# Edge network kernel: z of even and odd quarters in the two row halves of the array, sums behind all of z

## The reference

```python
h = jnp.maximum(_layernorm(x), 0.0)                       # 6250 x 64
msg_in = concat([h[src], h[dst], edge_attr_32], axis=-1)  # 206250 x 160
messages = silu(msg_in @ W1 + b1) @ W2 + b2
att = softmax(silu(msg_in @ Wa1 + ba1) @ Wa2 + ba2, axis=0)   # over all edges
agg = segment_sum(messages * att, dst, 6250)
out = x + silu(concat([h, agg], -1) @ Wu1 + bu1) @ Wu2 + bu2
```

## Time and profile before

| | |
|---|---|
| median of 3 runs | 2449.22 us (2447.33 to 2454.1) |
| profiled execution: span | 2482.0 us |
| profiled execution: its own time beside the span | not on record |
| POOL busy | 1529.9 us (62%) |
| PE busy, PEld busy | 1101.1, 963.4 us |
| DVE busy | 1086.6 us |
| ACT busy | 919.5 us |
| chain that ended last | issue 48%, PE 33%, DVE 9% |

### The profile page before, as it was taken

The page is one execution under the profiler, slowest core; times in us unless marked ns, Lnnn a source line. Parts: engine busy times, 40 slices in busy tenths (PEclk is TensorE's granted clock), DMA queues, the critical chain, the costliest instruction groups (busy, mean ns, idle before and its releaser), DMA issues.

```text
span 2482.0 us, 21022 instructions
## 1 busy us (share of the span) xinstructions
PE 1101.1 (44%) x6767; PEld 963.4 (39%) x6767; DVE 1086.6 (44%) x2367; ACT 919.5 (37%) x1107; POOL 1529.9 (62%) x1628
## 2 busy tenths in 40 slices
PE   4334444444444444444444444444444444444447
PEld 3223343444333333444333334343433333444444
DVE  4344444444444444444444444444444444444445
ACT  3333333334333333334333333343433333333433
POOL 4666666666666666666666666666666666666650
PEclk8566666666666666666666666666666666666766
DMA  7433333333333333333333333333333333333321
GB/s 202 106 90 90 90 89 88 92 91 95 98 93 88 90 88 88 90 93 90 99 95 89 89 90 89 87 94 89 98 95 91 89 90 90 87 93 90 95 65 27
DMA packets 101990, 228.43 MB, mean 92 GB/s; under 512 B 45184, under 2 KB 65460, under 8 KB 91636
## 3 DMA queue, kind: packets, MB, share of 16 engines
q1 hardware_dynamic: 47588, 120.63, 18.5%
q0 software_dynamic: 51584, 105.75, 17.2%
q10 hardware_dynamic: 2704, 0.66, 0.1%
HBM read 218.91 MB, written 8.00 MB: 91 GB/s over the span
## 4 chain that ended last, share of the span: by engine, by line
issue 48%; PE 33%; DVE 9%; another core or an unknown queue 7%; ACT 1%; SPq 1%; DVEq 0%; DMA 0%; ACTq 0%
PE bank L622 20%; PE bank L636 11%; DVE hot L865 2%; DVE v L902 2%; DVE bank L912 1%; DVE prod L895 1%; PE bank L732 1%; PE bank L722 0%; DVE lgb L921 0%; DVEq L875 0%; ACT comb L492 0%; PE bank L584 0%; ACT s L524 0%; PE bank L655 0%
## 5 line engine op out<-in xcount | busy, mean ns | idle before, releaser
L404 POOL DMA_INDIRECT p_rows<-p_tab,src_all x1612 | 1521.9, 944 | 872.3 <-issue 464.7
L622 PE MATMUL bank<-q_win,comb 128*128 128x128 f32 x3224 | 723.7, 369 | 981.9 <-issue 963.8
L622 PEld LDWEIGHTS bank<-q_win,comb 128*128 128x128 f32 x3224 | 643.9, 279 | 1099.1 <-issue 1095.4
L492 ACT ACTIVATE comb<-dst_b,row_of 96x1024 f32<-96x1024 int32 (+1 forms) x162 | 219.0, 1352 | 1336.6 <-PE bank L622 1227.8
L911 DVE TENSOR_TENSOR bank<-bank,p_rows 128x128 f32<-128x128 f32 x80 | 23.9, 299 | 1205.5 <-remote 672.6
L636 PE MATMUL bank<-hot,v 128*65 128x96 f32 x3200 | 320.1, 252 | 344.7 <-issue 274.8
L636 PEld LDWEIGHTS bank<-hot,v 128*65 128x65 f32 x3200 | 282.7, 141 | 342.1 <-issue 264.5
L912 DVE TENSOR_TENSOR bank<-bank,p_rows 128x512 f32<-128x512 f32 (+1 forms) x403 | 266.5, 666 | 71.7 <-PE bank L622 38.6
L524 ACT ACTIVATE s<-bank 128x512 f32<-128x512 f32 x403 | 232.1, 589 | 108.7 <-DVE bank L912 83.8
L498 ACT ACTIVATE comb<-comb,ones 96x1024 f32<-96x1024 f32 (+1 forms) x162 | 218.9, 1351 | 2.7
L865 DVE TENSOR_TENSOR hot<-bank,rel 128x960 f32<-128x960 f32 x162 | 178.3, 1139 | 0.0
(11 more groups left out here) (108 smaller groups left out, 304.0 us busy)
## 6 DMA issues: line engine op xcount, KB each, us to landing
dst_b<-dst_row SPq DMA_DIRECT2D x80, 960.0 KB
p_rows<-p_tab,src_all POOLq DMA_INDIRECT x1612
comb<-efT SPq DMA_DIRECT2D x80, 320.0 KB
q_win<-q_tab SPq DMA_DIRECT2D x81, 48.0 KB
p_tab<-s SPq DMA_DIRECT2D x12, 256.0 KB
q_tab<-s SPq DMA_DIRECT2D x12, 256.0 KB
out<-s SPq DMA_DIRECT2D x6, 256.0 KB, 2.3
x_sb<-x SPq DMA_DIRECT2D x2, 512.0 KB, 5.1
```

Source lines behind the costliest of these rows:

```text
L404: pool.indirect_dma_start(p_rows[:, a, t * H2:(t + 1) * H2], None, p_tab, bass.IndirectOffsetOnAxis(src_all[:, g * TG + t:g * TG + t + 1], ...
L492: nc.scalar.activation(comb[0:WIN, a, c0:c1], dst_b[:, c0:c1], ACT.Abs, bias=row_of[0:WIN, bass.ds(g, 1)]).then_inc(abs_ok, 1)
L622: last = nc.tensor.matmul(ps_z[q][:, (t % TQ) * H2:(t % TQ + 1) * H2], comb[:, a, t * P:(t + 1) * P], q_win[:, a, :], start=True, stop=True)
```

## The change

- A quarter's z takes 64 rows of the array: 32 nodes and the 32 edge features. Even quarters (0, 2, 4) lie in partitions 0 to 63, odd ones (1, 3) in 64 to 127, each with its own window of 32 nodes from the first receiver of the quarter. `comb` and dst_b hold up to three blocks of 512 edges a half, `q_win` three windows.
- `zmm` takes one or two quarters and alternates between them tile by tile; each goes into its own bank. Per group: quarters 0 and 1, then 2 and 3, then 4 alone.
- All of z of group g+1 stands ahead of sums of group g-1 (`z_ahead`).
- The one-hot is one DVE comparison over 128 partitions and 1536 columns (`own_nodes`), at the end of DVE's group, two groups ahead; Abs and Relu on ACT go. It writes all partitions of `comb`, so ef is loaded after it.
- SP issues five loads of 32 rows in place of one of 96 per group, and two DMAs each for ef and dst_b (one a half), dst_b over 32 partitions a half. In its list the windows of g+2 come when z of g is done, then, after own_nodes of g+2, dst_b of g+3 and ef of g+2.
- At the start ef of groups 0 and 1 is loaded after the tables are stored and after own_nodes, not between the two tables.
- The sums keep their window of 96 nodes. The check of the fit covers the quarters too. The host lays dst and ef out by halves.

```diff
-    WIN = P - DE
+    WIN = 96
+    QW = DE
+    HB = 2 * QW
...
+        def load_windows(eng, g, a):
+
+            for q in range(quarters(g)):
+                r = q % 2 * HB
+                node = eng.value_load(bases_i[0:1, bass.ds(NG + g * NQ + q, 1)], min_val=0, max_val=N - QW)
+                eng.dma_start(q_win[r:r + QW, a, q // 2, :], q_tab[bass.ds(node, QW), :]).then_inc(win_ld[a], 16)
 
         def load_ef(eng, g, a, s):
 
-            T = tiles(g)
-            eng.dma_start(comb[WIN:P, a, 0:T * P], efT[:, bass.ds(g * GE, T * P)]).then_inc(s, 16)
+            for h in range(2):
+                n = blocks(g, h) * QE
+                eng.dma_start(comb[h * HB + QW:(h + 1) * HB, a, 0:n], ef_h[h * QW:(h + 1) * QW, bass.ds(g * GH, n)]).then_inc(s, 16)
...
+                eng.dma_start(dst_b[h * HB:h * HB + QW, 0:n], dst_h[h:h + 1, bass.ds(g * GH, n)].broadcast_to([QW, n])).then_inc(dst_b_ld, 16)
...
             rows_stored(sp, 2 * (NB + 1))
-            load_window(sp, 0, 0)
-            load_window(sp, 1, 1)
-            sp.wait_ge(abs_ok, 2)
+            load_windows(sp, 0, 0)
+            sp.wait_ge(own_ok, 1)
             load_dst_b(sp, 1)
+            load_ef(sp, 0, 0, ef_ld[0])
+            load_windows(sp, 1, 1)
+            sp.wait_ge(own_ok, 2)
+            load_dst_b(sp, 2)
+            load_ef(sp, 1, 1, ef_ld[1])
 
             def load_group(g, a):
                 nxt2 = following(g)[1]
                 if nxt2 is not None:
-                    sp.wait_ge(abs_ok, 2 * g + 4)
-                    load_dst_b(sp, nxt2)
                     sp.wait_ge(z_done, (g + 1) * NQ)
+                    load_windows(sp, nxt2, a)
+                    sp.wait_ge(own_ok, g + 3)
+                    if nxt2 < LAST:
+                        load_dst_b(sp, nxt2 + 1)
                     load_ef(sp, nxt2, a, ef_ld[a])
-                    load_window(sp, nxt2, a)
...
                 for q in range(tiles(g) // TQ):
                     act.wait_ge(z_ok, g * NQ + q + 1)
                     nc.scalar.activation(silu_rows(a, q), halves(ps_z[q][:]), ACT.Silu).then_inc(silu_ok, 1)
-                    if q == 2:
-                        if g > 0 and not is_last(g):
-                            weights(g - 1, 1 - a)
-                        if nxt2 is not None:
-                            one_hot_abs(nxt2, a, 0)
-                    if q == 3 and nxt2 is not None:
-                        one_hot_relu(nxt2, a, 0)
-                    if q == 4 and nxt2 is not None:
-                        one_hot_abs(nxt2, a, 1)
-                        one_hot_relu(nxt2, a, 1)
+                    if q == 2 and g > 0 and not is_last(g):
+                        weights(g - 1, 1 - a)
...
+            def zmm(g, a, qs):
+
+                if qs[0] == 0:
+                    pe.wait_ge(ef_ld[a], per(a, g, 32))
+                    pe.wait_ge(win_ld[a], windows_landed(g))
+                wait(pe, silu_ok, (g - 1) * NQ + qs[-1] + 1)
+                for t in range(TQ):
+                    for q in qs:
+                        cols = slice(q // 2 * QE + t * P, q // 2 * QE + (t + 1) * P)
+                        last = nc.tensor.matmul(ps_z[q][:, t * H2:(t + 1) * H2], comb[half_rows(q), a, cols], q_win[half_rows(q), a, q // 2, :],
+                                                start=True, stop=True)
+                        if t == TQ - 1:
+                            last.then_inc(z_done, 1)
+
+            def z_ahead(g, a):
+
+                for qs in ((0, 1), (2, 3), (4,)):
+                    if qs[0] < quarters(g):
+                        zmm(g, a, [q for q in qs if q < quarters(g)])
...
             def group(g, a):
                 nxt = following(g)[0]
-                late = not (isinstance(g, int) and g == 0)
-                quarters = range(tiles(nxt) // TQ) if nxt is not None else []
-                for q in [q for q in (0,) if q in quarters]:
-                    zmm(nxt, 1 - a, q)
-                for q in [q for q in (1, 2) if q in quarters]:
-                    zmm(nxt, 1 - a, q)
-                if late:
+                if nxt is not None:
+                    z_ahead(nxt, 1 - a)
+                if g > 0:
                     sums(g - 1)
-                for q in [q for q in (3, 4) if q in quarters]:
-                    zmm(nxt, 1 - a, q)
...
+            def own_nodes(g, a):
+
+                n = blocks(g, 0)
+                dve.wait_ge(dst_b_ld, 32 * (g + 1))
+                wait(dve, z_done, (g - 1) * NQ)
+                nc.vector.tensor_tensor(comb[:, a, 0:n * QE].rearrange("p (k e) -> p k e", e=QE), dst_b[:, 0:n * QE].rearrange("p (k e) -> p k e", e=QE),
+                                        node_no[:, g, 0:n].unsqueeze(2).broadcast_to([P, n, QE]), ALU.is_equal).then_inc(own_ok, 1)
+            own_nodes(0, 0)
...
                     weighted(g - 1, 1 - a)
+                if following(g)[1] is not None:
+                    own_nodes(g + 2, a)
```

More of the change, by code:

```diff
@@ L22 @@
 EDGE_TILES = 20
+TILE = 128
 F32 = mybir.dt.float32
@@ L300, in _ @@
             sp.dma_start(x_sb[0:LT, NT - 1, :], x[(NT - 1) * P:N, :]).then_inc(x_ld[2], 16)
-            with nc.allow_non_contiguous_dma(reason="one dst of each group"):
-                sp.dma_start(first_i[:, 0:LAST], dst_row[:, 0:LAST * GE].rearrange("a (g e) -> a g e", e=GE)[:, :, 0]).then_inc(first_ld, 16)
-            sp.dma_start(first_i[:, LAST:NG], dst_row[:, LAST * GE:LAST * GE + 1]).then_inc(first_ld, 16)
+            with nc.allow_non_contiguous_dma(reason="one dst of each quarter"):
+                sp.dma_start(first_i[:], dst[0:1, ::TQ]).then_inc(first_ld, 16)
             sp.dma_start(src_all[:, 0:TG], src[:, 0:TG]).then_inc(src_ld[0], 16)
@@ L482, in _ @@
                     root(3, *PIECES[2])
[L484 to L504, removed]
             nc.scalar.activation(ref[:], ones[0:U1, 0:1].broadcast_to([U1, NP]), ACT.Copy, scale=LOW).then_inc(low_ok, 1)
@@ L596, in _ @@
                     pe.wait_ge(base_ok, 1)
-                    nc.tensor.matmul(ps_small[:, 0:NG], ones[0:1, :], base_f[:], start=True, stop=True).then_inc(baseB_done, 1)
+                    nc.tensor.matmul(ps_small[:, 0:NG + NQT], ones[0:1, :], bases_f[:], start=True, stop=True).then_inc(baseB_done, 1)
             for b in range(NB + 1):
@@ L611, in _ @@
             pe.wait_ge(q_ok, NB + 1)
[L613 to L621, removed]
-                    last = nc.tensor.matmul(ps_z[q][:, (t % TQ) * H2:(t % TQ + 1) * H2], comb[:, a, t * P:(t + 1) * P], q_win[:, a, :],
-                                            start=True, stop=True)
-                last.then_inc(z_done, 1)
+            def zmm(g, a, qs):
[14 more added lines that the diff above has]
+                        zmm(g, a, [q for q in qs if q < quarters(g)])
             def sums(g):
@@ L655, in own_part @@
                 nc.tensor.matmul(ps_u[b][0:rows_of(b), 0:n], wu1d[:, 0:rows_of(b)], hP[:, b * UT // 2 * P:b * UT // 2 * P + n], start=True, stop=False)
-            for q in range(NQ):
-                zmm(0, 0, q)
+            z_ahead(0, 0)
             groups(pe, group)
@@ L845, in worst_fit @@
             def worst_fit():
[L847 to L848 removed]
+                dve.wait_ge(rel_ok, 3)
+                chain(nc.vector.tensor_tensor(back[:, 0:LAST], bases_f[:, 0:LAST], bases_f[:, 1:NG], ALU.subtract))
                 chain(nc.vector.tensor_reduce(bad1[:, 0:1], back[:, 0:LAST], AX.X, ALU.max))
@@ L1009, in total_weight @@
                 nc.vector.tensor_scalar(wws[:], ww[:], rz[0:U1, :], None, ALU.mult).then_inc(scale_ok, 1)
+            own_nodes(1, 1)
             for g in range(LAST):
@@ L1143, with halves @@
     edges = np.concatenate([np.arange(full), np.arange(N_EDGES - last, N_EDGES)])
+    NG = -(-len(edges) // GE)
+    def halves(rows):
+        q = np.zeros((NG * GE, rows.shape[1]), rows.dtype)
+        q[:len(edges)] = rows
+        q = q.reshape(NG, -1, 4 * P, rows.shape[1])
+        q = np.stack([q[:, [0, 2, 4]], q[:, [1, 3, 3]]])
+        return q.transpose(0, 4, 1, 2, 3).reshape(2 * rows.shape[1], -1)
     src, dst, ef = (np.ascontiguousarray(inputs[n])[edges] for n in ("src", "dst", "edge_attr_32"))
@@ L1147 @@
         "dst": dst.reshape(-1, P).T,
-        "dst_row": dst.reshape(1, -1),
-        "efT": ef.T,
+        "dst_h": halves(dst[:, None]),
+        "ef_h": halves(ef),
     }
```

117 lines of the change are left out of this document (71 added, 46 removed).

## The result

Beside each other the kernel before took 2451.66 us (median of 4 runs) and the kernel after 2580.9 us (2573.8 to 2599.93): 5.4% slower, ratio 1.0538, 95% interval 1.0498 to 1.0579. The forecast was 2610. The profiled execution of after took 2579.75 us, its span is 2578.1.

The account below looks back on a forecast made before the run. TensorE, starved of instructions while gathers are issued, was taken to cause POOL's pause each group. +164 over 78 groups, +7 at the start, -8 at the end made 2645, less 33 for span over median: 2610 us, range 2400 to 2680.

Parts of the forecast that it names:

- The supply of TensorE: TensorE during gathers: about one instruction per us beyond a stock of some 120, refilled only when gathers stop.
- two groups per pause: POOL runs 40 gathers between pauses of 11 to 15 us; 31.5 us a group, chance 0.42, range 2530 to 2680.
- rival 1: POOL still pauses once per group, after 20 gathers: 29.0 to 30.7 us a group, 2425 to 2557 us; chance 0.30.
- The steady part and the last groups: Whole kernel: +2.1 us a group over 78 groups, +164; -8 for the last groups and their shorter z.
- Starving in sums, not in z: TensorE: sums, at the back of the queue, starve, show as single matmuls, and hold VectorE through `add_part`.
- Paired z: TensorE z in alternating 64-row halves: 0.14 us a record, 1.7 us of dense time saved a group, bounds 0 and 3.3.
- ScalarE: Abs and Relu go, 5.4 us a group; worth 0, at most 2.7 us.
- dst_b: DMA falls from 960 KB to 320 KB a group; worth 0, bounds 0 and -4.4 us a group.
- own_nodes: VectorE's new comparison of 128 x 1536: 1.8 us a group, costing 1.8 us a pause if its cover goes.
- SP: Five windows in place of one on SP: 1.07 us each, 5.3 us, early in the group and hidden.
- The start: SP's slow windows and ef delay z(0) to about 101 us, first addition to about 104: +7 us once.
- Rival 2: dst_b's transfers starve TensorE, so POOL's pause goes wholly or partly: 2106 us, half of it 2280; chance 0.17.

Follow-up runs that it names:

- e6: Kernel before with three of four gathers left out from group 2 on: 1200.12 us, one execution, beside 2477.62 for the kernel before.
- e12: Kernel after with the sums put back between z of quarters 2 and 3: 2506.9 us beside 2454.59 for the kernel before, ratio 1.0229.
- e11: Kernel before with only the order changed, all of z ahead of the sums: 2545.8 us beside 2452.11 for the kernel before, ratio 1.0381.
- e5: Kernel after, unchanged, run again in a set without creeping: 2109.46 us beside 2103.76 for the kernel before, ratio 1.0018.
- e1: Kernel before with all of z ahead of the sums, in a set without creeping: 2104.96 us beside 2106.12, ratio 0.9996.

## Why the prediction came out near, and what in it was wrong

**The supply of TensorE** as a count of instructions holds for after, and e6 bears out that it hangs on the gathers. Stretches of after between two returns of the pace (columns as in the earlier trace rows): the burst, the creeping and the 3.4 us of pause of one group, then four whole cycles.

```profile
1205.70:1212.10 6.40, 6.33 (x56) 5.79 (x55) 5.97 (x17) 2.74 (x4) 4.81 (x6) 0.75 0.57 155
1212.10:1230.50 18.40, 4.92 (x13) 3.40 (x14) 1.49 (x4) 3.03 (x6) 14.11 (x15) 0.60 0.21 55
1230.50:1233.90 3.40, 1.31 (x3) 0.78 (x3) 0.00 (x0) 0.00 (x0) 0.00 (x0) 0.50 0.08 19
1269.00:1298.20 29.20, 12.19 (x75) 10.40 (x75) 14.28 (x29) 5.94 (x9) 18.92 (x20) 0.62 0.26 71
1298.20:1327.50 29.30, 13.77 (x77) 12.11 (x77) 13.96 (x29) 5.94 (x9) 18.91 (x20) 0.62 0.19 48
1327.50:1357.00 29.50, 12.71 (x78) 10.84 (x77) 10.73 (x27) 5.94 (x9) 18.92 (x20) 0.62 0.26 70
1357.00:1389.90 32.90, 13.80 (x92) 12.24 (x93) 18.03 (x33) 5.94 (x9) 18.91 (x20) 0.60 0.31 83
```

111 records in the burst, 27 while creeping, 6 until the pace returns. The whole cycles hold 150, 154, 155 and then 185 records: three short of the 160 needed by 10, 6 and 5, and a fourth that catches up. The prediction's balance (128 + 15 + 18, which is 161 and is said to fit 160 "exactly") missed that rhythm. The kernel with the old order has it too. Four cycles of e12:

```profile
1069.80:1098.50 28.70, 12.85 (x74) 11.68 (x74) 14.14 (x29) 6.05 (x9) 18.93 (x20) 0.56 0.29 72
1098.50:1127.50 29.00, 12.81 (x75) 11.03 (x74) 14.18 (x29) 6.05 (x9) 18.91 (x20) 0.62 0.29 71
1127.50:1157.20 29.70, 14.07 (x80) 12.41 (x80) 14.18 (x29) 6.05 (x9) 18.91 (x20) 0.56 0.28 70
1157.20:1187.40 30.20, 16.01 (x97) 14.47 (x99) 14.25 (x30) 6.05 (x9) 18.91 (x20) 0.56 0.26 69
```

148, 149, 160 and 196 records. Here the catching up takes a cycle of 30.2 us in place of 28.7 to 29.7. In after it takes 32.9, elsewhere 35.1 (from 1233.9 to 1269.0 us, 184 records). This difference is the loss.

**The step that failed: "two groups per pause".** I expected "VectorE goes straight on into group g+1", additions 0 to 4 early, 40 gathers between pauses of 11 to 15 us. There are 20 between them, as rival 1 had it, and in 74 of 75 pauses POOL waits for addition 0 of a group. Here is why, VectorE's and TensorE's matmuls in order of time around the long pause:

```profile
1198.97 0.31 DVE L915 SCALAR_TENSOR_TENSOR acc<-acc,fade,bank 65x96 f32 x1 [14.82 <-remote]
...
1204.81 0.69 DVE L942 TENSOR_TENSOR bank<-bank,p_rows 128x512 f32<-128x512 f32 x1
...
1234.09 0.31 DVE L915 SCALAR_TENSOR_TENSOR acc<-acc,fade,bank 65x96 f32 x1 [20.50 <-remote]
...
1234.63 2.21 DVE L895 TENSOR_TENSOR hot<-bank,rel 128x960 f32<-128x960 f32 x2
...
1236.85 1.49 DVE L932 TENSOR_TENSOR v<-s,bank 128x1300 f32<-128x1300 f32 x1
1238.26 1.74 DVE L849 TENSOR_TENSOR comb<-dst_b,bank 128x1536 f32<-128x1536 int32 x1
1239.93 0.69 DVE L942 TENSOR_TENSOR bank<-bank,p_rows 128x512 f32<-128x512 f32 x1
```

```profile
1206.03 4.91 PE L646 MATMUL bank<-hot,v 128*65 128x96 f32 x40
1210.87 1.16 PE L625 MATMUL bank<-q_win,comb 64*128 64x128 f32 x14
1212.83 0.27 PE L625 MATMUL bank<-q_win,comb 64*128 64x128 f32 x1 [0.80 <-issue]
...
1233.95 2.12 PE L625 MATMUL bank<-q_win,comb 64*128 64x128 f32 x10 [1.03 <-issue]
1238.40 3.94 PE L646 MATMUL bank<-hot,v 128*65 128x96 f32 x23 [2.33 <-DVE v L932]
```

TensorE's records of sums end at 1211 us, but their semaphore is updated at 1233.95, and `add_part` behind it runs at 1234.09, after 20.50 us of idle time, and only then follow the one-hots, v and own_nodes and at last addition 0 at 1239.93. That tail is 1239.93 - 1234.09 = 5.84 us, and the pause is longer by 10.41 - 4.81 = 5.6. Ahead of the short pause the sums' signal came at 1198.83, before the gathers had ended (1200.96), and the same tail ran from 1198.97 to 1204.81. It was through just when z's signals came (1204.55), so it cost 0.3 us at most. In the long pause z's signals came at 1234.10 and VectorE could take addition 0 only at 1239.93: there the tail stands in the pause whole. In the old order z of quarters 3 and 4 stand last on TensorE, VectorE waits for these (L946, L911), and that tail comes behind the addition that POOL needs. So the order does not give POOL two groups; it puts 5.8 us of VectorE between TensorE's catching up and POOL. e11, which has no own_nodes in this tail, has shorter long pauses (8.05 against 9.38, own_nodes takes 1.74), and e12, which has it in the old order, none. The term "a group's tail on VectorE stands ahead of the restart" is in none of my cases; rival 1 came next with "VectorE's 1.8 us and its chain come in the pause", 30.7 us a group, against 30.5 measured. The total came out near by luck, because errors cancel. The steady part and the last groups were put at +164 - 8 and measured +70 - 2; the start at +7 and measured +28; and the 33 us by which before's span lies over its median were taken off, though after's span does not lie over its median. 88 too much, less 21, less 33: 34 by the terms, 29 by the medians. And 30.5 us a group is the near end of the case that failed; its far end, 34.2, would give some 2820 us, where its "own range" stops at 2680.

**Starving in sums, not in z**: wrong by the records, right in its effect. The single matmuls of after are z (L625): sums stand at the front of the queue when the burst comes, because z of the next group had crept through ahead of them. But the signal of these sums comes only behind the creeping stretch, in the long cycles when gathers have ended, and `add_part` is held by it, as forecast. The records alone do not say when the sums were done.

**Paired z**: 16 matmuls in 1.94 us (e5), 0.12 each; predicted 0.14. Worth nothing, as said. (The forecast's 3.3 us for a halved pace is a slip: 32 x 0.19 / 2 is 3.1.) **ScalarE** and **dst_b**: worth nothing, as said; e12's steady period shows it. **own_nodes**: 1.74 for 1.8, hidden but in the long pauses. **SP**: 12.1 us for five windows in place of the predicted 5.3, hidden all the same. **The start**: z(0) and the first addition of after:

```profile
95.47 5.69 SPq L302 DMA_DIRECT2D q_win<-q_tab  x5
...
105.98 4.76 PE L625 MATMUL bank<-q_win,comb 64*128 64x128 f32 x40 [13.25 <-DMA comb<-ef_h]
108.06 1.30 DVE L942 TENSOR_TENSOR bank<-bank,p_rows 128x512 f32<-128x512 f32 x2 [1.56 <-PE bank L625]
```

108.06 in place of 96.55 is +11.5 us, predicted +7; and the next groups, which have no stock of loads either, bring it to +28 at gather 200 (+18 in e12). **Rival 2** (dst_b makes TensorE starve) is out: after and e12 move a third of it and creep as long, and e6 moves all of it, in less than half the time, and does not creep behind 101 us. But its floor, 2106 us without pauses, is to the microsecond what the kernel before takes where TensorE does not creep. The Trainium skill (Runtime: NRT & Kernel Launch, Instruction fetch mechanics) says that fetching is mostly hidden; by that rule the change would give 0. In e5's set this is so (1.0018), in the first set it is not (1.0538).

**What stays open.** First, the cause of the creeping. Its traces differ in one more thing: the kernel before's (2482.0 us) holds 7,631 records of semaphore updates and e1's, of a program with as many instructions (2107.5 us), 34,249; after's holds 8,883 and e5's, of the same program, 41,657. Records are lost where TensorE creeps. Either one slow path delays both, or writing the records holds the engines up; no run here separates these, and so it is also open whether a use without any recording would creep. The transfers that the pages call "instruction" do not differ: 56 packets on q8 and 58 on q14 in before as in e1, 0.92 and 0.48 MB, and a packet of q8 takes 1.12 us in the one and 1.14 in the other. They are also fewer than the 81 groups on either queue. So the loading of instructions, once under way, is no slower; whether something behind it is, no trace shows. Second, e12 is 52 us slower than the kernel before by medians and 17 by the two traces, since the traced execution of before lies 33 us above its median. The 18 us at the start are seen, the other 34 are not placed. The same gap stands in after (129 by medians, 96 by traces) and in e11 (94, 56), so it seems to belong to the one trace of before and not to e12; a second trace of before in that condition would tell.

## What to carry to other kernels

Before an order of instructions is changed, ask for each engine's list what stands between the late signal and the instruction that the bottleneck waits for: here the sums' late completion was harmless until the order made the next group's first addition stand behind it and 5.8 us of VectorE. A stock that refills only in pauses is not spent at leisure; the pause ends with the first addition, not when the backlog is through. And time the kernel before beside every experiment: it took 2106 us in some sets and 2450 in others, and the change cost nothing or 5% accordingly.

## What the runs showed of the hardware

In the creeping condition a matmul's signal comes late as well. In after the last matmul of the sums shown above is recorded at 1210.70 us and the update of its semaphore at 1233.95. Over 27 groups between 900 and 1700 us the update stands 1 to 24 us behind the record in the 26 whose update is recorded, and in 18 of these exactly 30 or 31 matmul records behind it. In before the distance is 7 to 20 us in all 27 groups, and there it harms nothing, since `add_part` comes behind additions that wait longer. In e1 it is 0.26 us in each of 26 groups. A record of a matmul in such a trace is thus no proof that its result could be used: the waiting engine's own start is. SP is slowed too (12.13 us against 4.66 for the same five windows), VectorE is not: its tail from `add_part` to addition 0 takes 5.84 us in after and 5.83 in e5.
